# Graph attention of a two-layer block: eight phases in one sequence, the ramp in PSUM, neighbour terms added by GpSimd

## What is computed

```python
def gat_layer(x, adj, W, a_self, a_neigh, b):
    feat = jnp.einsum('nf,hfo->hno', x, W)
    attn_self = jnp.einsum('hno,ho->hn', feat, a_self)
    attn_neigh = jnp.einsum('hno,ho->hn', feat, a_neigh)
    e = attn_self[:, :, None] + attn_neigh[:, None, :]
    e = jax.nn.leaky_relu(e, LRELU_ALPHA)
    e = e + MASK_VAL * (1.0 - adj)[None, :, :]
    alpha = jax.nn.softmax(e, axis=-1)
    out = jnp.einsum('hnm,hmo->hno', alpha, feat) + b[:, None, :]
    out = jnp.transpose(out, (1, 0, 2)).reshape(out.shape[1], -1)
    return jax.nn.elu(out)
def per_graph(x, a):
    h = gat_layer(x, a, W0, a_self0, a_neigh0, b0)
    return gat_layer(h, a, W1, a_self1, a_neigh1, b1)
```

## Time and profile before

| | us |
|---|---|
| median of 3 runs (2323.64 to 2325.8) | 2325.22 |
| profiled execution, own time | 2323.65 |
| profiled execution, span | 2322.1 |
| PE busy | 1861.5 (80%) |
| DVE busy | 1542.1 (66%) |
| ACT busy | 1108.2 (48%) |
| POOL busy | 586.9 (25%) |
| mean granted TensorE clock (share of 2.4 GHz) | 0.897 |

### The profile page before, as it was taken

The page is one execution under the profiler, slowest core; times in us unless marked ns, Lnnn a source line. Parts: engine busy times, 40 slices in busy tenths (PEclk is TensorE's granted clock), DMA queues, the critical chain, the costliest instruction groups (busy, mean ns, idle before and its releaser), DMA issues. The chain is left out here.

```text
span 2322.1 us, 35149 instructions
## 1 busy us (share of the span) xinstructions
PE 1861.5 (80%) x8271; PEld 904.7 (39%) x8272; DVE 1542.1 (66%) x3266; ACT 1108.2 (48%) x2014; POOL 586.9 (25%) x701
## 2 busy tenths in 40 slices
PE   1788866888745999999993288888889629999994
PEld 0444433344342555555551122222222414444442
DVE  5988877888766555565563377777776485555552
ACT  1988857888632232232232246666666522222221
POOL 3000012000101555455542211111111003444441
PEclk9799876999876999999996579999999859999997
DMA  4100122001172778889655831111111537988884
GB/s 131 47 37 39 32 79 83 38 1 60 37 230 75 173 174 228 220 182 224 119 100 158 171 57 52 51 51 51 51 51 35 187 104 181 229 230 226 229 213 110
DMA packets 201022, 275.48 MB, mean 119 GB/s; under 512 B 83372, under 2 KB 121740, under 8 KB 199820
## 3 DMA queue, kind: packets, MB, share of 16 engines
q1 hardware_dynamic: 158731, 173.28, 24.3%
q0 software_dynamic: 38544, 97.02, 21.0%
q10 hardware_dynamic: 3633, 3.88, 1.0%
...
HBM read 204.44 MB, written 73.37 MB: 120 GB/s over the span
## 5 line engine op out<-in xcount | busy, mean ns | idle before, releaser
L1876 DVE TENSOR_REDUCE a_negmax<-a_m 128x1 f32<-128x512 f32 x512 | 328.1, 686 | 101.7 <-PE a_m L1732 100.1
L1824 ACT ACTIVATE a_prob<-a_s 128x1024 f32<-128x1024 f32 x256 | 260.4, 1020 | 142.9 <-PE a_s L1743 137.4
L1268 PE MATMUL f_gu_bank<-f_wgu,f_xT 128*128 x768 | 269.4, 494 | 6.8 <-issue 4.1
L1732 PE MATMUL a_m<-a_kT,a_qT 112*128 (+1 forms) x512 | 198.5, 399 | 82.6 <-DVE a_negmax L1876 39.0
L354 PE MATMUL g_pt<-g_ident,g_p 128*128 128x128 f32 x1024 | 185.6, 311 | 95.6 <-ACT g_p L460 94.2
L1268 PE MATMUL s_gu_bank<-s_wgu,s_xT 128*128 128x512 f32 x512 | 232.0, 596 | 2.3 <-ACT s_xT L1320 1.6
L354 PEld LDWEIGHTS g_pt<-g_ident,g_p 128*128 128x128 f32 x1024 | 127.7, 156 | 239.0 <-issue 151.3
L460 ACT ACTIVATE g_p<-g_e,g_emin 128x512 f32<-128x512 f32 x256 | 184.2, 720 | 66.0 <-DVE g_emin L554 65.9
L1234 POOL DMA_INDIRECT tokens<-f_y,f_ids x96 | 152.1, 1584 | 222.5 <-DMA tokens<-f_y,f_ids 176.6
L544 DVE SCALAR_TENSOR_TENSOR g_l<-g_tb,g_s,g_h 128x512 f32<-128x512 f32 x256 | 190.4, 745 | 17.2 <-ACT g_h L438 17.2
L1268 PEld LDWEIGHTS f_gu_bank<-f_wgu,f_xT 128*128 128x128 f32 x768 | 143.3, 191 | 138.6 <-issue 60.9
...
## 6 DMA issues: line engine op xcount, KB each, us to landing
...
```

Source lines behind the costliest of these rows:

```text
L1268: last = nc.tensor.matmul(gu_bank[k % TR][:, 0:F], xT[k % TR][:, c, :], wgu[:, bass.ds(place, 1), c, :].rearrange("p a f -> p (a f)"), sta ...
L1732: nc.tensor.matmul(m_bank[n % RING][:, :], qT[k][0:PAIR_ROWS, head, st * P:(st + 1) * P], group_keys(G, PAIR_ROWS, slice(0, N)), start=Tru ...
L1824: nc.scalar.activation(prob[n % QR][:, :, :], s_bank[n % RING][:, :, :], ACT.Exp).then_inc(p_ready, 1)
L1876: V.tensor_reduce(negmax[k % RING][:, st, head:head + 1], m_bank[n % RING][:, :], X_AXIS, ALU.max, negate=True).then_inc(m_read, 1)
```

## The change

The two turns become one sequence of eight phases, in the same order of phases, with nothing outside them but the start. In it:

- the ramp, now relu(4 (s + t)), goes to one of two PSUM banks (`g_h`), two units ahead; the other branch `g_l` is no longer computed on DVE. POOL adds mask and neighbours' terms to `g_near` for each unit (four buffers), and DVE's mask-and-minimum takes `g_near` and the ramp. A node's own term of the low branch is constant over a row and is dropped, since softmax does not see it;
- the transposes have two PSUM banks, and DVE makes all copies, three iterations behind (`COPY_LAG`);
- output, product, ELU exponential and sum live in one PSUM bank `g_o`; output steps are at units 4 to 7;
- mask statistics of graphs 1 to 3 lie in phases 0, 3 and 4 at units 16 to 19, normalisation on DVE at units 20 to 23, and POOL multiplies with 1e10 in one step per tile at its units 20 to 23; layer 1's weight products lie at units 4 to 11 of the first phase;
- loads at the start: layer 0's weights, vectors and contexts first, the first mask from ACT's queue, layer 1's weights last.

The diff, cut to its core:

```diff
-    TURNS = B // SLOTS
-    PHASES = 2 * SLOTS
+    PHASES = 2 * B
-    ACT_COPIES = (0, 2, 4, 6)
-    RELU_AHEAD, LOW_AHEAD = 4, 2
+    H_BANKS, PT_BANKS = 2, 2
+    COPY_LAG = 3
...
+    def mask_phase(m):
+        return m // SLOTS * 2 * SLOTS + m % SLOTS - 1
...
+                def load_mask(b):
+                    sp.wait_ge(near_ready, (mask_phase(b) + 1 - SLOTS + 1) * UNITS)
+                    sp.dma_start(mask[b % SLOTS][:, :, :], rows_of(b)).then_inc(x_in[b % SLOTS], 16)
...
+                def mask_tile(m, t):
+                    tile = mask[m % SLOTS][:, t, :]
+                    pool.wait_ge(adj_ready, m * NT + t + 1)
+                    pool.tensor_scalar(tile, tile, -1.0, 1e10, ALU.add, ALU.mult).then_inc(mask_ready, 1)
...
+                def add_neighbours(n):
...
+                    if n >= LAG:
+                        pool.wait_ge(e_ready, n - LAG + 1)
+                    pool.tensor_tensor(near[:, n % LAG, :], mask[slot][:, local % NT, :], t_all[k % SLOTS][:, local // NT, :], ALU.add).then_inc(near_ready, 1)
...
+                    if n < ALL_UNITS:
+                        add_neighbours(n)
+                    for m in range(1, B):
+                        t = n - mask_phase(m) * UNITS - 20
+                        if 0 <= t < NT:
+                            mask_tile(m, t)
...
+                def transposes(n):
+                    if n >= PT_BANKS:
+                        pe.wait_ge(pt_ready, n - PT_BANKS + 1)
+                    pe.wait_ge(p_ready, n + 1)
...
+                    if step == 4:
+                        pe.wait_ge(pt_ready, PAIR * (pr + 1))
+                        if pair == 0:
+                            pe.wait_ge(feat_ready, (k + 1) * NT)
+                        if pr:
+                            pe.wait_ge(h_ready, pr)
+                    if 4 <= step < 4 + NT:
...
+                def root(m):
+                    act.wait_ge(var_done, m + 1)
+                    nc.scalar.activation(std[:, m, :], std[:, m, :], ACT.Sqrt).then_inc(std_done, 1)
...
+                    if n >= H_BANKS:
+                        act.wait_ge(e_ready, n - H_BANKS + 1)
+                    nc.scalar.activation(h_bank[n % H_BANKS][:, :], t_all[k % SLOTS][:, h, :], ACT.Relu, scale=4.0,
+                                         bias=s_high[k % SLOTS][:, t, h:h + 1]).then_inc(high_ready, 1)
...
-                        V.scalar_tensor_tensor(out=lneg[:, n % LAG, :], in0=t_all[k % SLOTS][:, h, :], scalar=s_low[k % SLOTS][:, t, h:h + 1],
-                                               in1=high[:, n % LAG, :], op0=ALU.add, op1=ALU.subtract).then_inc(low_ready, 1)
...
+                    V.tensor_tensor_reduce(out=eneg[:, n % LAG, :], in0=near[:, n % LAG, :], in1=h_bank[n % H_BANKS][:, :],
+                                           scale=-1.0, scalar=3.0e38, op0=ALU.add, op1=ALU.min,
+                                           accum_out=emin[:, n % LAG:n % LAG + 1]).then_inc(e_ready, 1)
...
+                    if step == PAIR:
+                        dve.wait_ge(rall_ready, pr + 1)
+                        dve.wait_ge(pv_done, pr + 1)
+                        V.tensor_tensor(o_bank[:, :], o_bank[:, :], rall[:, :], ALU.mult).then_inc(z_ready, 1)
...
+                for n in range(ALL_UNITS + 2 * PAIR):
+                    if n < ALL_UNITS:
+                        masked(n)
+                    if COPY_LAG <= n < ALL_UNITS + COPY_LAG:
+                        copy_probT(n - COPY_LAG)
+                    if n >= 2 * PAIR:
+                        finish(n // PAIR - 2, n % PAIR + PAIR)
+                    if n >= PAIR and n < ALL_UNITS + PAIR:
+                        finish(n // PAIR - 1, n % PAIR)
+                    if n // UNITS + 1 < PHASES:
+                        prepare(n // UNITS + 1, n % UNITS)
+                    if 4 <= n < 4 + 2 * FC:
+                        weigh(2 + (n - 4) // FC, (n - 4) % FC)
...
+                        step = n - mask_phase(m) * UNITS - 16
+                        if step == 0:
+                            mask_statistics(m)
```

697 lines of the change are left out of this document (325 added, 372 removed).

## The result

| | before | after |
|---|---|---|
| median of the runs | 2325.51 us (2323.64 to 2326.94, 4 runs) | 2361.14 us (2357.4 to 2362.5, 4 runs) |
| ratio, 95% interval | | 1.0151 (1.0134 to 1.0169) |
| span of the profiled execution | 2322.1 | 2360.5 |
| mean granted clock | 0.897 | 0.887 |

The change makes the kernel 1.5% slower. The forecast was 2347.4, slower by 22; measured is slower by 35.6. The direction and the main mechanism hold, but several terms of the sum are wrong and partly cancel. Two slow executions in the last batch are left out of the ratios: one of 2983.83 us of the kernel before and one of 6808.63 us of the kernel with four edits.

What follows compares the result with a forecast made beforehand. Bound: DVE (89% busy), with PE and ACT nearly full, so waits between them would end a unit. Terms -21.4 - 43.2 + 11.0 + 61.8 + 4 + 10 = +22.2 us on 2325.2 gave 2347.4; range 2285 to 2400.

Steps and rivals of the forecast that it cites:

- Bound and mechanism: Head pairs: DVE, with less work, stands 2.9 us in every pair before its product, waiting for PE's last output step.
- Start: Before the first mask-and-minimum: layer 0's products come first, so it starts at about 37 instead of 58.40; -21.4 us.
- Boundary: Between the two turns: one sequence removes the 45.2 us gap, less one unit of 2.0; -43.2 us.
- Part 3, products: Units 4 to 11: layer 1's eight multiply-reduce couples on DVE, each 2 x 0.69, without cover; +11.0 us.
- the rivals, at 0.03: POOL and DVE block each other: every addition holds up a DVE instruction, a pair takes 22 us, total 2470; chance 0.03.
- Part 4, POOL's step: Masks 1 to 3, units 20 to 23: add-multiply takes 2.54 us; DVE stands 4 x 4.0 = 16.0 us per mask.
- cheap mask step: POOL's mask step: add-multiply is priced like multiply-add, 23 us less, total 2324, no change; chance 0.20.
- during this PE catches up: Masks 1 to 3: PE catches up while DVE stands, so the next waits (2.9 and 0.9) vanish; -3.8 us each.
- Parts 5 and 6, pairs and clock: Eight phases of head pairs: 522 us against 518, +4; slower clock in output steps of 18 light pairs, +10.
- Rule against rows: Mask-and-minimum reading PSUM: profile rows show no surcharge, the skill's fixed cycles would add 17 us (2365); the sum follows the rows.
- last rival: POOL and DVE block each other (0.03); quoted rule: VectorE with two SBUF inputs and GpSimd reading SBUF exclude each other.
- the faster side: Light pairs: DVE's standing is covered as PE's output steps finish before the product; 52 us less, 2295; chance 0.17.

Runs made afterwards that it cites:

- the kernel with four edits: Changed kernel with product, maximum and ELU later, mask steps at units 24 to 27, layer 1's products before the loop, square root behind ELU exponential: 2273.84 us, ratio 0.9783.

## Why the prediction was right, and where it was not

- **Bound and mechanism: right.** DVE, relieved of work, waits for PE's last output step: 2.9 us a pair forecast, 85.8 / 30 = 2.9 measured. That the figures agree to the digit is luck, since single waits run from 1.84 to 5.40 us; that the wait stands in every pair is not. Moving the product by 1.22 us took 1.22 off it in light pairs.
- **Start: right**, 4 us better. Traffic did not hold up the neighbour terms as long as assumed: they are asked for at 24.67 and first used at 31.44, 6.8 us later, not at 35.8. **Boundary: right** as far as the gap goes.
- **Part 3, products: mis-sized**, 11.0 against 15.9. The price of 0.69 came from the earlier trace rows, where POOL is idle. Beside POOL's additions a multiply takes 1.37: 8 x 0.68 = 5.4 more. That stood among the rivals, at 0.03, since POOL's own rows looked the same with DVE busy and idle. They could not show it: the instruction that starts later is held up, and in the changed kernel that is DVE's multiply, 0.44 us behind the addition.
- **Part 4, POOL's step: the failed choice.** I took 2.54 us, by the order (add, multiply) and the dearer single multiply of the earlier trace rows. It takes 0.62, like (multiply, add). Each of 12 waits is 2.06 instead of 4.0: 23 us too much. The *cheap mask step* among the rivals (0.20) came true in its mechanism; its time of 2324 did not, as the other terms were too low.
- **Part 4, "during this PE catches up" (-3.8 a mask): wrong**, 11 us too little. The product at unit 24, right after four such waits, still waits 3.00 us. PE's last transposes need the copy that DVE does just before the product, so what is waited for is always at least one unit of PE's work behind that copy. PE, idle so long, had half its clock in units 20 to 22, where output steps took 1.98, and unit 23's transposes and output step still lay behind that copy; these are the output step of unit 22, unit 23's two and the product:

```profile
107.64 1.98 PE L397 MATMUL g_o<-g_pT,g_feat 128*64 128x512 f32 x4
...
111.42 0.82 PE L365 MATMUL g_pt<-g_ident,g_p 128*128 128x128 f32 x4
...
112.17 1.08 PE L397 MATMUL g_o<-g_pT,g_feat 128*64 128x512 f32 x4
...
113.36 0.70 DVE L559 TENSOR_TENSOR g_o<-g_o,g_rall 128x512 f32<-128x512 f32 x1 [3.00 <-PE g_o L397]
```

  With the step at its true price and nothing absorbed, the terms give 16.6 a mask (5.4 + 3.0 + 4 x 2.06); 16.6 to 18.0 were measured.
- **Parts 5 and 6, pairs and clock: mis-sized**, 14 against 30. About 10 is the boundary's: before, the first pair of the second turn took 375.67 - 363.32 = 12.35 with nothing behind it, and the last 7 units of the first 318.08 - 306.75 = 11.33 with nothing ahead. In one sequence both are full pairs: 375.55 - 358.87 = 16.68 and 358.87 - 339.39 = 19.48, that is 4.3 and, less the unit of 2.0 that the boundary's term counts, 6.1 more. I took away the gap and forgot that fill and drain were cheap units beside it. Some 13 (12.7) lie in the four phases that prepare a layer 1: 69.6 and 75.7 us instead of 68 and 71, where I had added only 0.2 and 0.7. What sets these pairs was not tried apart. The light pair was too low as well: 15.5 and 16.7 against 14.8 and 15.2. It gained nothing on the kernel before: the 16 for layer 1, from 61.9 / 31 x 8, is a mean with the cheap last units, and single light pairs took 16.3 to 16.9. In layer 1 the residual addition and the product both wait, 1.74 and 1.84, where I had 2.7 for both. The clock fell where PE stands, as forecast, but in light pairs in units 2 to 4, not in the output steps; worth some 6 to 8 us, forecast 10, which is close by luck.
- **Rule against rows:** for the mask-and-minimum from PSUM the rows decided right: 674 ns, no surcharge. The multiplies went by the rule that the prediction quotes under its last rival.
- **A slip:** the rival *the faster side* decides once PE's four steps cost less than 3.7 - 0.2 = 3.5 us, not 3.7 + 0.2; its 0.9 a step is from the right figure.

So -23 for the step, and -4 for the start, stood against +11, +16 and +5: the forecast came closer than its terms, by luck.
